# Windowed attention of a six-layer network: scores laid out with the head pair's parity in the partitions, and the turned probabilities copied in two 64x512 operations a group

## The reference, cut to what matters

```
HEADS, DIM_HEAD, WINDOW = 16, 64, 32
q, k, v = split(x @ Wqkv)            # 16 heads of 64
q, k = l2norm(q) * qs, l2norm(k) * ksc, then rotary embedding
# window w: its 32 queries see the 64 keys of windows w-1 and w
mask = (it < jb) | (it > jb + w) | (jb == -1)
sim = einsum('bhwie,bhwje->bhwij', bq, bk2) * 8.0
attn = softmax(where(mask, -max, sim), -1)
out = einsum('bhwij,bhwje->bhwie', attn, bv2)
x = out.reshape(b, n, 1024) @ Wo + x
```

## Time and profile before

| | |
|---|---|
| time, median of 3 runs | 1858.16 us (1856.6 to 1858.77) |
| the profiled execution: span from its first to its last instruction | 1854.4 us |
| PE busy | 1671.0 us (90%) |
| DVE busy | 1659.0 us (89%) |
| ACT busy | 1513.9 us (82%) |
| POOL busy | 1529.7 us (82%) |

### The profile page before, as it was taken

The page is one execution under the profiler, slowest core; times in us unless marked ns, Lnnn a source line. Parts: engine busy times, 40 slices in busy tenths (PEclk is TensorE's granted clock), DMA queues, the critical chain, the costliest instruction groups (busy, mean ns, idle before and its releaser), DMA issues.

```text
span 1854.4 us, 59361 instructions
## 1 busy us (share of the span) xinstructions
PE 1671.0 (90%) x19888; PEld 1365.4 (74%) x19888; DVE 1659.0 (89%) x3652; ACT 1513.9 (82%) x3170; POOL 1529.7 (82%) x1079
## 2 busy tenths in 40 slices
PE   5789999899999899999899999989999989999995
PEld 4567777777777777777777777767777777777773
DVE  6799999999999999999999999999999999999972
ACT  3578888888888888888888888888888888888882
POOL 3498988888898799889889988988898889889870
PEclk9899999999999999999999999999999999999997
DMA  5110110001101000300010310001201000100110
GB/s 140 45 31 22 28 31 20 20 28 54 61 28 31 20 20 28 95 20 25 23 31 20 92 31 20 20 28 31 84 28 27 24 20 28 31 20 20 29 33 24
DMA packets 29943, 65.43 MB, mean 35 GB/s; under 512 B 4948, under 2 KB 16216, under 8 KB 29144
## 3 DMA queue, kind: packets, MB, share of 16 engines
q1 hardware_dynamic: 29912, 65.03, 12.2%
HBM read 19.93 MB, written 1.05 MB: 11 GB/s over the span
## 4 chain that ended last, share of the span: by engine, by line
PE 46%; ACT 30%; issue 14%; DVE 6%; ACTq 2%; POOL 1%; SPq 0%; DMA 0%; DVEq 0%; POOLq 0%
PE bank L1026 35%; PE bank L1151 6%; ACT pz L601 5%; ACT qz L584 5%; ACT sq L562 3%; ACT es L592 3%; ACT L592 3%; ACT L623 3%; PE bank L1180 3%; ACT ot L608 2%; DVE w_lo L811 1%; ACT ht L629 1%; ACT x_hi L555 1%; PE bank L1222 1%; ACT ht L630 1%
## 5 line engine op out<-in xcount | busy, mean ns | idle before, releaser
L395 POOL TENSOR_TENSOR rot<-t 128x512 f32<-128x512 f32 x384 | 491.9, 1291 | 162.4 <-DVE t L837 162.4
L405 POOL TENSOR_TENSOR rnorm<-n2c,minus_half 128x16 f32<-128x16 f32 x192 | 577.0, 3005 | 16.0 <-DVE n2c L848 0.8
L601 ACT ACTIVATE pz<-bank 64x256 f32<-64x256 f32 x768 | 289.8, 377 | 51.8 <-PE bank L1180 36.4
L834 DVE TENSOR_TENSOR t<-bank,rtab 128x512 f32<-128x512 f32 x384 | 260.9, 679 | 56.4 <-ACT sq L562 41.9
L1026 PE MATMUL bank<-w_hi,x_hi 128*128 128x512 f32 x576 | 282.1, 490 | 9.5 <-DVE t L837 6.0
L418 POOL TENSOR_TENSOR es<-es,r 128x512 f32<-128x512 f32 x192 | 200.7, 1045 | 94.5 <-DVE r L878 94.5
L839 DVE TENSOR_REDUCE n<-sq 128x8 f32<-128x512 f32 x384 | 259.6, 676 | 0.0
L1151 PE MATMUL bank<-ident,rot 128*128 128x128 f32 x1536 | 237.4, 277 | 23.5 <-ACT qz L584 10.6
L562 ACT ACTIVATE sq<-bank 128x512 f32<-128x512 f32 x384 | 224.6, 596 | 16.5 <-PE bank L1026 13.1
L584 ACT ACTIVATE qz<-bank 64x512 f32<-64x512 f32 x384 | 225.7, 588 | 10.0 <-PE bank L1151 5.2
L1026 PE MATMUL bank<-w_hi,x_lo 128*128 128x512 f32 x576 | 229.9, 399 | 0.0
(11 more groups left out here) (102 smaller groups left out, 3543.8 us busy)
## 6 DMA issues: line engine op xcount, KB each, us to landing
vb<-v SPq DMA_DIRECT2D x96, 384.0 KB, 3.4
w_new<-in_Wqkv SPq DMA_DIRECT2D x6, 1536.0 KB, 8.6
vb<-v SPq DMA_DIRECT2D x48, 128.0 KB, 2.3
w_o<-in_Wo SPq DMA_DIRECT2D x6, 512.0 KB
w<-in_W SPq DMA_DIRECT2D x6, 341.0 KB
b<-in_b SPq DMA_DIRECT2D x6, 341.0 KB
out<-acc SPq DMA_DIRECT2D x1, 1024.0 KB, 5.1
w<-in_W SPq DMA_DIRECT2D x12, 64.0 KB
```

What stands on the lines that cost most here:

```text
L395: g.tensor_tensor(rot[:, i * CH:(i + 1) * CH], t1[:, b:b + CH], t2[:, b:b + CH], ALU.add)\
L405: g.tensor_tensor(rnorm[:, w], n2c[:, w], minus_half[:, :], ALU.pow).then_inc(s_rn, 1)
L601: a.activation(pz4[64 * s:64 * s + 64, u % 2, odd::2, s, :], src[64 * odd:64 * odd + 64, :, s, :], ACT.Copy).then_inc(s_pte, 1)
L834: d.tensor_tensor(heads(t1[:, b:b + CH]), src, table(n, kind, T), ALU.mult).then_inc(s_t1, 1)
```

## The change

The scores of window s and pair p move. Before, window s chose the half of the partitions, and the pair the 64 columns. Now the pair's parity chooses the half of the partitions, and the columns are (pair // 2, s, key). One 128-column block then holds one window's keys next to the other's, and its transpose has (s, key) in the partitions and (parity, head in pair, query) in the columns. So window s's keys stand in the partitions 64s to 64s+63 already, and `take_p` is one copy 64x512 for each window. `pz` becomes (buffer, s, head, query), and `values` reads a head's two pieces 512 columns apart. The mask table has 4 x 64 columns instead of 2 x 64, since the first window of a sequence is now told by the column and not by the partition. In `scores` the sixteen 64x64 products stand in the same order of pair and window as before, but the half that they write to changes after every second product.

```
-        mask = sb("mask", 2 * 64, BF16)
-        maskf = sb("maskf", 2 * 64)
+        mask = sb("mask", 4 * 64, BF16)
+        maskf = sb("maskf", 4 * 64)
...
-        pz4 = pz[:, :].rearrange("p (b a s c) -> p b a s c", b=2, a=PAIRS, s=2)
-        pz5 = pz[:, :].rearrange("p (b a s h q) -> p b a s h q", b=2, a=PAIRS, s=2, h=2)
+        pz4 = pz[:, :].rearrange("p (b s c) -> p b s c", b=2, s=2)
+        pz5 = pz[:, :].rearrange("p (b s h q) -> p b s h q", b=2, s=2, h=HEADS)
...
                 act.wait_ge(s_pt, nth(4, n, u + 1))
                 act.wait_ge(s_av, nth(4, n, u - 1))
-                src = pP[:, :].rearrange("p (a s c) -> p a s c", a=4, s=2)
-                for odd in range(2):
-                    for s in range(2):
-                        a.activation(pz4[64 * s:64 * s + 64, u % 2, odd::2, s, :],
-                                     src[64 * odd:64 * odd + 64, :, s, :], ACT.Copy).then_inc(s_pte, 1)
+                for s in range(2):
+                    r = slice(64 * s, 64 * s + 64)
+                    a.activation(pz4[r, u % 2, s, :], pP[r, :], ACT.Copy).then_inc(s_pte, 1)
...
                 mm(pS[:, :], identh[:, :],
-                   mask[:, first * 64:first * 64 + 64].unsqueeze(1).to_broadcast([P, PAIRS, 64]),
+                   mask[:, first * 128:first * 128 + 128].unsqueeze(1).to_broadcast([P, PAIRS // 2, 128]),
                    stop=False)
                 for pair in range(PAIRS):
+                    odd = pair % 2
                     for s in range(2):
                         w = 4 * T + al + 2 * s
-                        last = mm(pS[64 * s:64 * s + 64, pair * 64:pair * 64 + 64],
+                        c = (pair // 2) * 128 + s * 64
+                        last = mm(pS[64 * odd:64 * odd + 64, c:c + 64],
...
-                pe.wait_ge(s_pte, nth(16, n, 4 * u))
+                pe.wait_ge(s_pte, nth(8, n, 2 * u))
...
-                pe.wait_ge(s_pte, nth(16, n, 4 * u + 4))
+                pe.wait_ge(s_pte, nth(8, n, 2 * u + 2))
...
-                              pz5[:, u % 2, pair, :, hh, :])
+                              pz5[:, u % 2, :, h, :])
...
-    first = seen & ((np.arange(P)[:, None] >= 64) | (j[None, :] >= WIN))
-    masks = np.where(np.concatenate([seen, first], 1), 0.0, MASKED).astype(f)
+    first = seen & (j[None, :] >= WIN)
+    masks = np.where(np.concatenate([seen, seen, first, seen], 1), 0.0, MASKED).astype(f)
```

## The result

The changed kernel takes 1828.27 us, the median of four runs (1826.77 to 1829.68), against 1857.95 (1856.60 to 1858.77) for the kernel before on the same chip. The ratio is 0.9839, with an interval of 0.9827 to 0.9851: 29.7 us faster. That lies in the stated range of 1787 to 1838, but not in the forecast's own range, which ended at 1821: the gain is 30 us where 55 were forecast. It is nearer to rival 1's 1835 than to 1803.

A forecast was written before the change was run, and what follows sets the result against it. PE and DVE, the busiest engines, lose their last 2 us an iteration to waits, mostly for ACT. Savings of 0.78 + 0.39 = 1.17 us, 47 times, make 55: 1854.4 - 55 + 3.8 = 1803 us, range 1787 to 1838.

The forecast's parts named there:

- rival 1: Across the iteration, the gain is half eaten by the next wait, earlier PE standing before DVE or POOL: 1835 us, chance 0.19.
- The copies: In take_p on ACT, two 64x512 copies replace four 64x256: 588 ns each, 0.39 us less a group, 75 us of ACT.
- Places B and C: Behind take_p(m,3), PE gains 0.39 of its 0.52 us wait; behind take_p(m,2), DVE gains 0.39 of 0.87, PE nothing.
- the sum: Savings on the path of each iteration: 0.78 + 0.39 = 1.17 us, 47 times, 55 us.
- Place A: PE's 1.24 us wait before values(n,1) for ACT's copy ot: two groups' savings remove 0.78, leaving 0.46.
- DVE can follow PE's 1.17: Over the iteration, DVE keeps up with PE's 1.17 us gain, taking that much out of its 2.66 us idle.
- the rest of the iteration slides forward with PE: Between the late places ACT itself restarts behind PE (a 0.34 us wait), so everything there moves earlier along with PE.
- next late would be DVE: After the change, DVE is the next engine to be late, 33.1 us busy in an iteration of 34.6.
- The scores' order: In scores, halves changing after every second product cost 0 if PE passes over six instructions; upper bound 0.93 us a group.
- rival 2: In scores, passes run strictly in program order: 0.52 us more a group, no change at 1858 us, chance 0.07.
- Rival 3: In scores, no two passes overlap any more: 0.93 us more a group, 1934 us, chance 0.06.
- The masks and the stride of `values`: Mask broadcast and larger table cost 0 (bound 1.9 us); values' 32 passes stay at 1.15 us despite distance 512.

The follow-up runs named there:

- The first experiment: Kernel before with take_p's four copies replaced by two contiguous 64x512 copies in every group, right placing of the probabilities left out: 1820.82 us, ratio 0.9812.
- the third experiment: Changed kernel with all eight score products of one half of the partitions first, then the other half's eight: 1859.22 us, ratio 1.0019 to the kernel before.
- The first two experiments: Short copies alone in the kernel before, 1820.82 us; alternating score halves in the changed kernel, 1821.54; the change's score order in the kernel before, 1856.75.

## Why the prediction was right, and where it was wrong

- **The copies: right.** A copy takes 589 ns (reckoned 588). The first experiment shows that they alone make the whole gain. Two in a row take 1.21 us against 1.58 to 1.59 for four, so 0.38 a group where ACT works without a gap. Over the span ACT lost 62 us and not 75, since in the mean of all groups the busy time fell by (289.8 - 226.1)/192 = 0.33.
- **Places B and C: right in size, by luck in part.** 18 us reckoned, 20 measured. But the wait at B fell by 0.20 to 0.25 and not by 0.39; another 0.20 came at A, which the sum had not linked with B and C.
- **Place A: wrong in size.** 37 us reckoned, 17 measured. The wait for `ot` went as it was said to, even further, from 1.24 to 0.23 or 0.40, where 0.46 was to stay. The step that failed is "DVE can follow PE's 1.17 (it needs that much out of 2.66 idle)" and with it "the rest of the iteration slides forward with PE". It compared totals over the iteration, which the prediction's first paragraph had warned of. DVE's idle time lies at its waits for ACT; in the ten microseconds ahead of `xm` it had 0.75 us before, and none after. The prediction did write "next late would be DVE", and did not go on to ask at which instruction. DVE's rows ahead of each product that PE would now reach sooner would have shown it.
- **The scores' order: costed at 0, measured at 0.05 us a group**, 5 us of the kernel once the waits that cover it are gone, 0 before. The guess on the engine was nearly right: PE does pass over six instructions (three passes and their weight loads), and what is lost is one moment of 0.058 us in seventeen. With passes strictly in the order of the program, rival 2, a group would have grown by 0.52, to 1.67 us; it took 1.20. The Trainium skill ("TensorE: Matmul & The Clock Gate", Part 3) says that matmuls start and end strictly in program order, and the change's rows don't agree with it. Nor do those of the third experiment, though there most passes run one by one. Strict order would leave one pair at the change of half, and there are three.
- **Rival 3: its mechanism exists, its time was wrong.** The third experiment leaves three pairs in 32 passes, 0.75 us more a group than before the change, and gives 1859, not the 1934 of the working. A pass more of PE's work is not a pass more of the iteration: the idle time left took 1.3 of the 2.8 us, and another 0.7 did not show in PE's busy time. The point from which it decides, 0.5 us a group, was set too low: at 0.75 the time is about that of the kernel before.
- **Rival 1: the outcome.** The gain was half eaten by the next wait, and it came from DVE, as it said. Its number, 1835 by way of the chain's 5% for `pz`, is 7 us off the measured time, and its way to it names no place; that it comes near is luck. It deserved more than 0.19. It is also its value, as the upper end of the stated range, that makes the range hold the result.
- **The layer boundaries: not in the sum.** Forty-seven iterations were taken as alike. The ten at the boundaries gained 1.9 us where the sum had 11.7. Part of it is that the clock fell at four boundaries and not at one; by the differences above, I estimate 3 us for it. PE's longer wait for `gt` is the other part that the rows show. The two weren't separated.
- **The masks and the stride of `values`: right at nothing.** The first two experiments together show it.

Added up per ordinary iteration: 1.17 forecast, 0.71 came, 0.49 more when `xm` and the order of the scores are mended. Over the span, 28.9 us shorter: the 34 ordinary iterations gave 25.2 us (39.8 in the sum), the ten at the boundaries 1.9 (11.7), the start and the end 1.8 (3.5).

## What to carry to other kernels

When a wait on a path is shortened, follow the waiting engine to its next waits and read, for each, when the engine that must serve it there can be done: idle time elsewhere in the loop is no slack at that place. A short producer that stands behind a long instruction on a full engine, as `xm` behind the sums here, is a thing to try first; here the move showed no gain until the other wait was gone. Price an edit of a full engine by the waits that it fills as well as by its busy time, and treat the iterations at a change of stage as a case of their own.

## What was not expected of the hardware

**A small instruction of DVE that takes six times as long.** `n2c` touches 128x16 elements. Its mean was 444 ns in the kernel before, 580 after, 289 in the kernel with short copies in groups 2 and 3, while the shortest take 160 to 170. Both engines' timeline in the kernel before:

```profile
957.64 1.05 POOL L412 TENSOR_TENSOR rot<-rot,rnorm 128x512 f32<-128x512 f32 x1
957.71 1.02 DVE L848 TENSOR_SCALAR n2c<-n 128x16 f32<-128x16 f32 x1
```

It starts just after POOL's product and ends with it, at 958.73 and 958.69. That is no single case: 47 of the 192 `n2c` take over 0.5 us in the kernel before and 79 in the change, and every one of them ends 0.03 to 0.04 us behind the end of a POOL product of 128x512. It looks as if DVE gets nothing done until POOL is through; the times alone say so, no experiment removed POOL's instruction. `n2c` has 26.0 us more in the change (111.3 against 85.3), more than DVE's whole rise of 19.9. So DVE was not given more work: one instruction, the same in size and number, is caught by one of POOL's products more often (79 times instead of 47).

**PE looks ahead over three waiting passes of one half, and not over four.** With the halves alternating, two by two, and eight by eight, the same 32 passes start at 16, 17 and 29 moments, and take 1.15, 1.20 and 1.90 us. Whether the weight loads between the passes count in that reach wasn't tried.

**The clock can fall behind a stop of 2 us, and need not.** At the boundary shown, a stop of 2.13 us was followed by 3.4 us at a granted clock of 0.5. The same stop of 2.13 us was followed by a fall at three of four boundaries, and one of 2.51 at the fifth. In the kernel before, the stops of 1.41 to 1.44 us for `gt` had none behind them; its one fall came 1.8 us after another stop, of 1.95 us for `qz`, which had none behind it at the other four boundaries.
